# The convolution's rows laid channel by channel, and a shorter TensorE warm-up, in a two-layer FFN kernel

## The reference, cut to what matters

```python
out = lax.conv_general_dilated(x, weight, window_strides=(1,), padding=[(4, 4)],
                               dimension_numbers=('NCH', 'OIH', 'NCH'), feature_group_count=4)
ctx = jnp.einsum('nd,od->no', c, c_weight)
conv = out + ctx[:, :, None] + bias[None, :, None]

x = x + (conv @ W.T + b + lora(conv))
x = x + L1_ffn(L1_cond(x, cond_128))
```

## Time and profile before

| | before |
|---|---|
| median of 3 executions | 658.79 us (657.31 to 658.83) |
| the profiled execution's own time | 658.74 us |
| its span in the profile | 656.9 us |
| PE busy | 649.5 us, 99% of the span |
| DVE busy | 451.2 us, 69% |
| ACT busy | 213.3 us, 32% |
| DMA | 157.98 MB, mean 240 GB/s |

### The profile page before, as it was taken

How to read it: one execution, slowest core, us unless ns; L and a number is a source line. 1 busy time by engine, 2 the same in 40 slices (tenths; PEclk the granted TensorE clock), 3 DMA queues, 4 the chain that set the end, 5 groups by cost and what they waited for, 6 DMA issues and landing times.

```text
span 656.9 us, 8354 instructions
## 1 busy us (share of the span) xinstructions
PE 649.5 (99%) x3197; PEld 537.6 (82%) x3197; DVE 451.2 (69%) x690; ACT 213.3 (32%) x275; POOL 73.1 (11%) x91
## 2 busy tenths in 40 slices
PE   9999999999999999999999999999999999999997
PEld 8878888888897788888788788888879888888875
DVE  2859569549377798468769658637868857656765
ACT  2714134333144125335134212334313311334510
POOL 1499300000000250000000051000000000000000
PEclk9999999999999999999999999999999999999999
DMA  8577715975969826777975672374986764047585
GB/s 306 206 291 273 303 49 156 354 234 208 397 230 394 331 107 281 273 219 275 358 267 214 260 292 96 129 214 156 385 319 243 290 248 165 0 137 230 193 335 199
DMA packets 51594, 157.98 MB, mean 240 GB/s; under 512 B 5488, under 2 KB 6384, under 8 KB 51568
## 3 DMA queue, kind: packets, MB, share of 16 engines
q1 hardware_dynamic: 46240, 148.05, 61.7%
q10 hardware_dynamic: 5328, 9.61, 4.7%
HBM read 131.94 MB, written 25.71 MB: 240 GB/s over the span
## 4 chain that ended last, share of the span: by engine, by line
PE 89%; DMA 6%; DVE 3%; issue 1%; SPq 1%; ACT 0%; DVEq 0%; POOL 0%; POOLq 0%
PE bank L1374 23%; PE bank L1376 23%; PE bank L1375 23%; PE bank L1388 9%; DMA piece_lo<-kept 6%; PE bank L1408 3%; PE bank L1395 2%; PE bank L1414 1%; PE bank L1400 1%; PE bank L1402 1%; PE bank L1415 1%; PE bank L1370 1%; DVE x L925 1%; DVE u_lo L1012 1%; DVE work L932 1%
## 5 line engine op out<-in xcount | busy, mean ns | idle before, releaser
L893 DVE TENSOR_TENSOR piece_lo<-raw,piece_hi 128x1024 fp32r<-128x1024 f32 x60 | 74.2, 1240 | 93.2 <-ACT piece_hi L646 93.2
L646 ACT ACTIVATE piece_hi<-raw 128x1024 fp32r<-128x1024 f32 x60 | 63.3, 1057 | 148.0 <-PE bank L1376 102.7
L1374 PE MATMUL bank<-piece_hi,u_hi 128*128 128x512 f32 x272 | 107.9, 397 | 0.1
L1375 PE MATMUL bank<-piece_lo,u_hi 128*128 128x512 f32 x272 | 107.3, 395 | 0.0
L1376 PE MATMUL bank<-piece_hi,u_lo 128*128 128x512 f32 x272 | 107.3, 395 | 0.0
L1374 PE MATMUL bank<-v_hi,piece_hi 128*128 128x512 f32 x256 | 101.8, 398 | 0.0
L1376 PE MATMUL bank<-v_hi,piece_lo 128*128 128x512 f32 x256 | 101.1, 395 | 0.0
L1375 PE MATMUL bank<-v_lo,piece_hi 128*128 128x512 f32 x256 | 101.0, 394 | 0.0
L1374 PE MATMUL bank<-piece_hi,v_hi 128*128 128x512 f32 x192 | 76.3, 397 | 1.8 <-DMA piece_lo<-kept 1.4
L1376 PE MATMUL bank<-piece_hi,v_lo 128*128 128x512 f32 x192 | 75.8, 395 | 0.0
L1375 PE MATMUL bank<-piece_lo,v_hi 128*128 128x512 f32 x192 | 75.7, 394 | 0.0
(11 more groups left out here) (143 smaller groups left out, 799.4 us busy)
## 6 DMA issues: line engine op xcount, KB each, us to landing
raw<-pieces SPq DMA_DIRECT2D x76, 512.0 KB, 5.5
piece_hi<-kept SPq DMA_DIRECT2D x48, 512.0 KB, 5.3
piece_lo<-kept SPq DMA_DIRECT2D x48, 512.0 KB, 6.3
x<-x SPq DMA_DIRECT2D x16, 512.0 KB, 5.1
gate_x<-gates ACTq DMA_DIRECT2D x32, 256.0 KB
out<-x SPq DMA_DIRECT2D x32, 256.0 KB, 4.4
conv_in<-conv_x SPq DMA_DIRECT2D x15, 516.0 KB, 6.7
conv_in<-pieces SPq DMA_DIRECT2D x12, 512.0 KB, 8.5
```

The costliest lines, as they stand in the source:

```text
L646: act.activation(piece_hi[:, n % SLOTS, :], raw[:, r % RAWS, :], ACT.Copy).then_inc(s_piece_hi, 1)
L893: dve.tensor_tensor(piece_lo[:, n % SLOTS, :], raw[:, r % RAWS, :], piece_hi[:, n % SLOTS, :].bitcast(F32), ALU.subtract).then_inc(s_piece ...
L1374: pe.matmul(to, left_hi, right_hi, start=first, stop=False)
L1375: pe.matmul(to, left_hi, right_lo, start=False, stop=False)
```

## The change

`conv_x` is laid out on the host with the phase outside and the channel inside, as before; now the loads read its rows so that on the partitions the channel is outside and the phase inside (partition = 8 x channel + phase). `load_conv_in` and `load_first` get a new helper for that, `conv_rows`, whose source has three levels, 16 channels x 8 phases x the row, in place of two. `load_taps` reads its windows in the same order: its outer loop now has 16 runs in place of 8. The bytes, the number of loads, their length per row and what is computed stay the same. `WARM_UP` is 8 in place of 12.

```diff
-WARM_UP = 12
+WARM_UP = 8
...
-            windows = bass.AP(taps.tensor, taps.offset + cg * CI * ci, [[tap, PH], [ci, CI], [1, 2 * P]])
+            windows = bass.AP(taps.tensor, taps.offset + cg * CI * ci, [[ci, CI], [tap, PH], [1, 2 * P]])
...
+            def conv_rows(g, t, start, width):
+                row = conv_x.shape[3]
+                return bass.AP(conv_x.tensor, conv_x.offset + (g * NT + t) * P * row + start,
+                               [[row, CI], [CI * row, PH], [1, width]])
...
             def load_conv_in(g, t):
                 sp.dma_start(conv_in[:, 2 * t:2 * t + 2].rearrange("p b g q -> p (b g q)"),
-                             conv_x[bass.ds(g, 1), t].rearrange("a p n -> (a p) n")).then_inc(s_convin[t], 16)
+                             conv_rows(g, t, 0, 2 * CG * (Q + 1))).then_inc(s_convin[t], 16)
...
                 sp.dma_start(conv_in[:, b].rearrange("p g q -> p (g q)"),
-                             conv_x[0, 0, :, b * width:(b + 1) * width]).then_inc(done, 16)
+                             conv_rows(0, 0, b * width, width)).then_inc(done, 16)
```

## The result

The changed kernel takes 666.8 us (median of 6 executions, 665.1 to 667.8) against 658.4 us for the kernel before on the same chips (6 executions). The ratio is 1.0119, 95% interval 1.0101 to 1.0137: 1.2% slower (the ratio on record isn't the quotient of the two medians, which is 1.0127). I had forecast 657.9 us, in a range up to 659.6.

A forecast was written before the change was run, and what follows sets the result against it. The prediction took TensorE's own work as the bound, busy 649.5 us of 656.9 us. The profiled 658.74 us less 0.89 us at the start gave 657.85, by the median 657.9 us, range 656.0 to 659.6 us.

The forecast's parts named there:

- the new row order: Input loads: up to 0.4 us more issue on the first load, hidden; the 15 later 516 KB loads cost nothing.
- The third rival: Rows 66 KB apart slow the input loads, weight pieces arrive late, TensorE waits: 662.2 us as upper end; chance 0.06.
- threshold of 1.9 times: From 1.9 times the input load time on, four loads overrun 4.7 us of free DMA time and weight pieces come late.
- The removed warm-up: Kernel start: eight records fewer save 1.71 us, slower convolution records give back 0.81 us, net 0.89 us.
- a sign of being wrong: The prediction would be wrong if, near the start, L1449 waited for `consts`.
- The second rival: Start: clock rises at another time; as early as 4.56 us, 2.0 us gained in sum, 656.8 us; chance 0.12.
- The landings: Start: `first_consts` lands at 6.4, batch 1 at 6.7, `hidden_w` at 6.9 us, all before they are needed.
- The first rival: Start: late data or the exponential's tie leaves a gain of 0 to 0.35 us, 658.4 to 658.8 us; chance 0.22.
- the term of 1.5 us: Start: taps on 16 engines instead of 8 free 1.5 us on the eight engines that the other loads also pass.
- the lead: The 0.89 us won at the start, expected to survive to the end of the kernel.
- the tie at 24 us: First large product waits for ACT's exponential, ending at 24.14 us exactly with the convolution; ACT's steps should move along.

The follow-up runs named there:

- the stored order: Host stores the input rows channel by channel, loads in two levels, taps in 16 runs, 8 warm-up matmuls: 659.3 us, ratio 1.0001 to the kernel before.
- The one with 12 warm-up matmuls: Input stored channel by channel by the host, two-level loads, taps in 16 runs, WARM_UP 12 in place of 8: 658.3 us, ratio 1.0007 to the kernel before.
- group 1 alone: The change's 16 x 8 split only for group 1's four input loads, other groups stored channel by channel in two levels: 663.4 us, ratio 1.0083 to the kernel before.
- the piece in front: The changed kernel with the weight piece between group 1's input loads issued in front of them: 668.1 us, ratio 1.0167 to the kernel before.
- the spare rows: Rows stored adjoining, a spare row behind each eight, so the source keeps the change's three levels of 16 x 8: 669.5 us, ratio 1.0155 to the kernel before.
- the halved loads: The changed kernel with each 516 KB input load made as two of 258 KB, rows of 2064 bytes: 664.5 us, ratio 1.0097 to the kernel before.

## Why the prediction was wrong

**The step that failed** is the one on the new row order: the 15 loads "move the same rows in another order, onto 16 engines as before: nothing, under the cover of the DMA time that is free". They cost two thirds more time per packet (267 ns for 160), and I had costed their form only at the issue on SP, where it is indeed 0.6 us for 0.43 and hidden. I had asked how many engines a load uses, and took it that their rate stays whatever the split. The trace of before had no input load with 16 outer runs, so there was no row for its price; the bounds from both sides that such a case wants (from nothing up to a load twice as long) I gave to a rival with a chance of 0.06 instead of to the term itself.

**The third rival was right in its mechanism** (the input loads get slow, weight pieces behind them come late, TensorE waits) and wrong in three points. Its cause, rows 66 KB apart, is refuted: eight adjoining rows are as slow. Its threshold of 1.9 times is refuted: 392/251 = 1.6 times was enough, since I compared the added DMA time with the free time of a stretch of 15 us at group 2, while the order of the list decides: the piece between the input loads comes late however free the microseconds after it are. And at group 1, the dearer place, I hadn't looked at all; there the DMA share was 1.03 before the change (172 to 180 us). And its price, 4.3 us at most, left out that a waiting TensorE comes back at the lower clock: the record-by-record difference has 4.9 + 1.8 us at group 1 and 2.4 + 1.2 us at group 2.

**The removed warm-up.** 16 records at 0.213 us and the first convolution record near 4.56 us (4.68) came as worked out. L1449 stands at 7.60 us, forecast was 7.61, but that is luck. TensorE's records go over to a distance of 0.112 us at 6.3 us, not at about 7.0, so the convolution was done sooner than worked out; then L1449's weights waited for `first_consts`, which I had named as a sign of being wrong:

```profile
7.60 0.19 PEld L1449 LDWEIGHTS bank<-consts 128*64 128x64 f32 x2 [0.28 <-DMA consts<-first_consts]
```

**The second rival** was right in that the instant moves: by the distance of TensorE's records the clock rises between 3.9 and 7.1 us in the 14 traces (6.9 before, 5.2 in the stored order). Its gain of up to 2.0 us took the data to be there, and they aren't. In the stored order TensorE reached the taps sooner, waited 0.8 us for them and 0.2 us for `hidden_w`, and L1451 stands at 8.36 us, as late as in the shorter warm-up alone (8.34), where the clock rose at 6.1. Where the clock rose early, the landings set this place, and the 2.0 us weren't there to be had.

**The landings.** `first_consts` was forecast at 6.4 us and landed at 2.36 + 5.2 = 7.6, `hidden_w` at 6.9 and landed at 3.37 + 5.0 = 8.4. So L1456 started at 8.41 us, not 7.82, and the first large product at 23.87 us, 0.37 us sooner than before in place of the forecast 0.9. The first rival had this right, 0.35 us. The times to landing, in the changed kernel:

```profile
consts<-first_consts ACTq DMA_DIRECT2D x1, 153.5 KB, 5.2
...
gate<-hidden_w SPq DMA_DIRECT2D x1, 128.0 KB, 5.0
```

The taps do go to all 16 engines now, as the Trainium skill's page "DMA: Bandwidth & Descriptors" (section "Why a DMA increments its semaphore by 16 and not by 1") has it for 16 outer runs: each taps load ends with 16 small semaphore packets in the trace, with 8 before. What failed is the term of 1.5 us: `first_consts` lands 0.3 us sooner than before (7.6 for 7.94), and was issued 0.28 us sooner, so its transfer gained next to nothing; `hidden_w` lands no sooner at all (8.4 for 8.36). From 3 to 6 us, after and then before:

```profile
3.00:6.00 3.00, 3.00 (x15) 2.83 (x14) 0.00 (x0) 0.00 (x0) 0.00 (x0) 1.00 1.03 304
```

```profile
3.00:6.00 3.00, 3.00 (x16) 3.00 (x15) 0.00 (x0) 0.00 (x0) 0.00 (x0) 1.00 0.88 232
```

Before, the other eight engines weren't idle for long either (0.88), and with all 16 busy on rows of 1 to 2 KB they move 304 GB/s, 19 each where I had 22. But the stored order, which has the taps in 16 runs too, moves 236 GB/s at a share of 0.88 in this stretch, so not even the 304 are due to the taps alone; why 16 engines bring so little here stays open. Of ten kernels with 8 warm-up matmuls and taps in 16 runs, eight were ahead at 79 us by 0.3 to 0.9 us, and two, with a later `hidden_w`, were 0.6 and 2.1 us behind.

**Does the lead survive?** Not past 190 us. I had looked at the tie at 24 us only; there the exponential moved along. The joint of group 0 and group 1 (164 to 190 us, where the last products of the one meet the convolution of the other) is what doesn't move: there TensorE waits for additions behind weight pieces, the DMA share is 1.0 from 164 to 180 us in the kernel before too, and all the versions with fast loads stand 1.2 to 2.8 us further back behind it, laid beside the one profiled execution of before. The one with 12 warm-up matmuls does too (2.6 us), and its median is that of before; so how much of this is the lead given back and how much the scatter of single executions stays open. Their ratios, 0.9994 to 1.0007, show no gain; a lead of 0.9 us would be 0.9986, which some of the intervals still hold, so it can't be ruled out for each of them, only not told. Left aside is the shorter warm-up alone, with 1.0041.

## What to carry to other kernels

When a load's access pattern changes, its price isn't known from the number of bytes, the row length and the number of engines: look for a load of the same split in the trace, and if there is none, keep the whole range in the forecast, or measure one. Here 16 outer runs of eight rows cost a third of the bandwidth where 32, 64 or 128 cost nothing; storing the array in the order wanted by the kernel cost the kernel nothing. And the wait that a slower transfer causes is to be sought behind it in the lists: a cheap addition that stands behind a late split held TensorE for 4.8 us, and moving the one piece only brought up the next.

## What the runs showed of the hardware that I had not expected

- Loads to 128 partitions whose source has 16 outer runs of eight rows move 251 to 261 GB/s with all engines at a share of 1.0 (7 to 16 us of four kernels); with 32, 64 or 128 outer runs the same bytes go at 377 to 397 GB/s. It doesn't depend on whether the eight rows adjoin in DRAM, nor much on rows of 2 or 4 KB (272 GB/s with halves). How the rows of a split are dealt out to the engines, and whether the reading or the writing side is what is slow, the traces don't show, so why 16 runs are slow stays open; I haven't tried it on stores.
- Transfers queued among them suffer too: a weight piece took 13.7 us from issue to landing instead of 8.4.
- Waits of 4.8 and 2.2 us of TensorE (the change), 3.5 us (group 1 alone), 3.8 us (the piece in front) and 1.1 us (the spare rows) were each followed by a stretch at the lower clock; those of 2.9 and 1.2 us (the halved loads), 2.1 us (the piece in front, near 312 us) and 1.8 and 1.3 us (the rows' order alone) were not. The length of the wait alone doesn't tell.
